# Attention stage of a two-layer model on one core: the state copy and the head gather move between engines, the scan units and value products are re-ordered

## The reference, cut to what matters

```python
def step(h, inp):                       # the scan of the Mamba block
    d_t, B_t, C_t, x_t = inp
    dA = jnp.exp(d_t[..., None] * A)
    dBx = d_t[..., None] * B_t[:, None, :] * x_t[..., None]
    h = h * dA + dBx
    y = jnp.sum(h * C_t[:, None, :], axis=-1)
    return (h, y)
...
A = jnp.einsum('bhnd,bhmd->bhnm', q, k) / jnp.sqrt(jnp.float32(Dm))
A = jnp.where(mask[None, None], A, -jnp.inf)
A = jax.nn.softmax(A, axis=-1)
sa = jnp.einsum('bhnm,bhmd->bnhd', A, v).reshape(Bm, Nm, Dm)
```

## Time and profile before

| | us |
|---|---|
| median of 3 runs | 2713.05 |
| the profiled execution | 2705.79 |
| its span | 2703.9 |
| TensorE busy | 2446.1 (90%) |
| VectorE busy | 2319.0 (86%) |
| ScalarE busy | 1859.3 (69%) |
| GpSimd busy | 1873.5 (69%) |

### The profile page before, as it was taken

How to read it: one execution, slowest core, us unless ns; L and a number is a source line. 1 busy time by engine, 2 the same in 40 slices (tenths; PEclk the granted TensorE clock), 3 DMA queues, 4 the chain that set the end, 5 groups by cost and what they waited for, 6 DMA issues and landing times. The chain is left out here.

```text
span 2703.9 us, 72872 instructions
## 1 busy us (share of the span) xinstructions
PE 2446.1 (90%) x29430; PEld 1463.3 (54%) x29430; DVE 2319.0 (86%) x2551; ACT 1859.3 (69%) x4077; POOL 1873.5 (69%) x1739
## 2 busy tenths in 40 slices
PE   7999999899777887899989999999999999999997
PEld 4444444333233334566656666666666666666665
DVE  6667778969898896899967899989998999899994
ACT  4555545466555553777767888888888888788883
POOL 2441142227767766677748899989998999999991
PEclk9999999999999998999989999999999999999999
DMA  3000000001121111030021112111211121111111
GB/s 104 9 9 9 9 7 9 8 23 40 49 49 44 49 47 39 7 94 14 12 64 47 38 31 66 37 32 35 62 33 36 35 62 40 29 32 37 33 22 38
DMA packets 171132, 97.57 MB, mean 36 GB/s; under 512 B 97155, under 2 KB 167791, under 8 KB 169263
## 3 DMA queue, kind: packets, MB, share of 16 engines
q1 hardware_dynamic: 170799, 92.91, 14.4%
HBM read 66.91 MB, written 7.08 MB: 27 GB/s over the span
## 5 line engine op out<-in xcount | busy, mean ns | idle before, releaser
L599 PE MATMUL ps<-xnT,qp 128*128 128x512 f32 (+3 forms) x1280 | 571.4, 565 | 28.4 <-ACT prob L814 28.3
L814 ACT ACTIVATE prob<-ps,mneg,shift 128x1024 f32<-128x1024 f32 (+7 forms) x384 | 366.3, 955 | 278.2 <-DVE mneg L720 277.3
L1902 DVE TENSOR_TENSOR area<-ps,tab 128x2048 f32<-128x2048 f32 x192 | 430.3, 2282 | 63.7 <-ACT area L1682 38.5
L720 DVE TENSOR_REDUCE mneg<-ps 128x1 f32<-128x1024 f32 (+7 forms) x384 | 341.1, 889 | 102.5 <-PE ps L599 101.6
L1413 PE MATMUL ps<-wqk,area 128*128 128x512 f32 x768 | 359.1, 610 | 27.9 <-DVE area L1968 22.4
L728 DVE STREAM_TRANSPOSE area<-prob 128x1024 f32<-128x1024 f32 (+7 forms) x384 | 354.1, 923 | 34.3 <-ACT prob L814 30.3
L2089 POOL TENSOR_TENSOR area<-area,rn 128x1024 f32<-128x1024 f32 x192 | 370.0, 1948 | 7.5
L1503 PEld LDWEIGHTS ps<-wvo,area 128*128 128x128 f32 x3072 | 355.2, 193 | 26.7 <-issue 20.9
L1503 PE MATMUL ps<-wvo,area 128*128 128x128 f32 x3072 | 361.9, 276 | 3.4 <-ACT area L1731 3.4
L599 PEld LDWEIGHTS ps<-xnT,qp 128*128 128x128 f32 x1280 | 222.2, 197 | 216.0 <-issue 167.0
L1724 ACT ACTIVATE ps<-ps,nmxl 128x64 f32<-128x64 f32 x1536 | 322.5, 344 | 5.1 <-DVE nmxl L1882 5.0
(11 more groups left out here) (273 smaller groups left out, 4445.1 us busy)
## 6 DMA issues: line engine op xcount, KB each, us to landing
xe<-bc_scratch SPq DMA_DIRECT2D x128, 128.0 KB, 3.1
area<-bc_scratch SPq DMA_DIRECT2D x128, 128.0 KB, 4.2
staged<-values_scratch SPq DMA_DIRECT2D x192, 32.0 KB, 1.9
wqk<-lwqk_dram SPq DMA_DIRECT2D x6, 1024.0 KB, 6.8
xp<-xc SPq DMA_DIRECT2D x96, 48.0 KB, 2.7
xc<-xs SPq DMA_DIRECT2D x96, 32.0 KB
wvT<-lwvT_dram SPq DMA_DIRECT2D x6, 512.0 KB, 8.1
wo<-lwo_dram SPq DMA_DIRECT2D x6, 512.0 KB, 9.7
```

Source lines behind the costliest of these rows:

```text
L599: mm = E.matmul(ps[:, r + o // 512, 0:w], k.qp[:, group % 2, i * P:(i + 1) * P], k.xnT[:, k0 + o:k0 + o + w], start=o // 512 != masked, st ...
L720: V.tensor_reduce(k.mneg[:, U:U + 1], of, X_AXIS, ALU.max, negate=True).then_inc(s("top"), 1)
L814: A.activation(k.prob[:, U % 2, 0:nk], ps[:, r:r + 2, :].rearrange("p a b -> p (a b)")[:, 0:nk], ACT.Exp, bias=k.mneg[:, U:U + 1], scale=k ...
L1902: V.tensor_tensor(k.rot[:, n % 2, w, :, :].rearrange("p c (h d) -> p c h d", d=DH), bcast(heads(what, n), 1, 2), bcast(k.tab[:, n % FRAME, ...
```

## The change

1. `shares`: the value products stand in whole groups of four: 4, 4, 4, 4, 4, 4, 8 for a square (before 4, 4, 4, 5, 5, 5, 5) and 0, 4, 4, 4, 4, 8, 8 for a triangle (before 2, 3, 4, 5, 5, 6, 7).
2. ScalarE's `values_out` is gone. VectorE turns the sums out of PSUM in 32 x 32 blocks (`turn_values`), and `gather` needs 4 products with the constant `pick` as the weights and 64 columns each, in place of 32.
3. The copy of the state moves from VectorE (L492) to ScalarE (`unit_state`), behind the exponential of the next step's odd piece; GpSimd's outputs wait for it.
4. GpSimd makes the input of unit u before the outputs of unit u - 1.
5. ScalarE makes the decay of unit u in the even piece of the same step, in place of the odd piece of the step before.
6. The scan starts at step 59 in place of 61, what prepares it comes one or two steps earlier, and the last two visits one step earlier.

```diff
-VISITS = {..., 50: ("dt", 0), 52: ("dt", 1), 98: ("mo", 0), 127: ("mo", 1)}
-FIRST_SCAN = 61
+VISITS = {..., 50: ("dt", 0), 51: ("dt", 1), 97: ("mo", 0), 126: ("mo", 1)}
+FIRST_SCAN = 59
...
-    return (4, 4, 4, 5, 5, 5, 5) if is_square(b) else (2, 3, 4, 5, 5, 6, 7)
+    return (4, 4, 4, 4, 4, 4, 8) if is_square(b) else (0, 4, 4, 4, 4, 8, 8)
...
 def unit_scan(k, u):
+    if c:
+        V.wait_ge(s("state"), u - NS + 1)
     for a in range(ET):
         ...
-    ins.then_inc(s("v"), k.v.up())
-    V.wait_ge(s("v"), k.v.n)
-    V.tensor_copy(k.last[:, i, :], k.hx[:, b, :, CH - 1]).then_inc(s("scanned"), 1)
+    ins.then_inc(s("scanned"), 1)
+
+def unit_state(k, u):
+    A, s = k.ac, k.sem
+    A.wait_ge(s("scanned"), u + 1)
+    A.activation(k.last[:, u % NS, :], k.hx[:, u % 2, :, CH - 1], ACT.Copy).then_inc(s("state"), 1)
...
     def gather(b):
         E.wait_ge(s("ot"), b + 1)
-        for i in range(NTH):
-            for q in range(4):
-                mm = E.matmul(ps[WIN * q:WIN * (q + 1), 6 + b % 2, 256 + DV0 * i:256 + DV0 * (i + 1)], k.oT[:, b % 2, WIN * i:WIN * (i + 1)],
-                              k.pick[:, DV0 * q:DV0 * (q + 1)], start=True, stop=True, skip_group_check=True)
+        of = k.oT[:, b % 2, :].rearrange("p (i q v) -> p q i v", q=4, v=DV0)
+        for q in range(4):
+            mm = E.matmul(ps[WIN * q:WIN * (q + 1), 6 + b % 2, 256:256 + DV0 * NTH], k.pick[:], of[:, q, :, :], start=True, stop=True, skip_group_check=True)
...
+    def turn_values(b):                       # VectorE, after the maximum in the first slot of batch b + 2
+        V.wait_ge(s("value_mm"), b + 1)
+        if b >= 2:
+            V.wait_ge(s("pick_mm"), b - 1)
+        V.transpose(k.oT[:, b % 2, :], ps[:, 6 + b % 2, 0:WIN * NTH]).then_inc(s("ot"), 1)
...
-        if i == 0 and b >= 2:                 # ScalarE
-            values_out(b - 2)
-        elif i == 2 and b >= 2:
+        if i == 2 and b >= 2:
             gathered(b - 2)
         j = step_of(U)
         if j is not None:
             branch(j)
-        elif U >= FIRST and scanned_in(step_of(U - 1) + 1) is not None:
-            A.wait_ge(s("half_pool"), at["pool"]["du"])
-            unit_decay(k, scanned_in(step_of(U - 1) + 1))
+            if scanned_in(j) is not None:
+                A.wait_ge(s("half_pool"), at["pool"]["du"])
+                unit_decay(k, scanned_in(j))
+        elif U >= FIRST and scanned_in(step_of(U - 1) - 1) is not None:
+            unit_state(k, scanned_in(step_of(U - 1) - 1))
...
     def outputs(u):                           # GpSimd
+        G.wait_ge(s("state"), u + 1)
         unit_outputs(k, u)
...
             branch(j)
+            if scanned_in(j) is not None:
+                unit_inputs(k, scanned_in(j))
             if scanned_in(j - 1) is not None:
                 outputs(scanned_in(j - 1))
-            if scanned_in(j) is not None:
-                unit_inputs(k, scanned_in(j))
```

More of the change, by code:

```diff
@@ L343, in up @@
         return 1
-VISITS = {8: ("sa", 0), 10: ("out", 0), 17: ("hat", 0), 19: ("in", 0), 21: ("in", 1), 23: ("in", 2), 25: ("in", 3), 47: ("xd", 0), 50: ("dt", 0), 52: ("dt", 1),
-          98: ("mo", 0), 127: ("mo", 1)}
-FIRST_SCAN = 61
+VISITS = {8: ("sa", 0), 10: ("out", 0), 17: ("hat", 0), 19: ("in", 0), 21: ("in", 1), 23: ("in", 2), 25: ("in", 3), 47: ("xd", 0), 50: ("dt", 0), 51: ("dt", 1),
+          97: ("mo", 0), 126: ("mo", 1)}
+FIRST_SCAN = 59
 TAP_ROWS = range(22, 45)
@@ L486, in unit_scan @@
         ins = V.tensor_tensor_scan(h, k.dc[:, b, a, :], h, k.last[:, i, a:a + 1] if c else 0.0, ALU.mult, ALU.add)
-    if c + 1 == NCH:
-        ins.then_inc(s("scanned"), 1)
-        return
-    ins.then_inc(s("v"), k.v.up())
-    V.wait_ge(s("v"), k.v.n)
-    V.tensor_copy(k.last[:, i, :], k.hx[:, b, :, CH - 1]).then_inc(s("scanned"), 1)
+    ins.then_inc(s("scanned"), 1)
[3 more added lines that the diff above has]
+    A.activation(k.last[:, u % NS, :], k.hx[:, u % 2, :, CH - 1], ACT.Copy).then_inc(s("state"), 1)
 def unit_outputs(k, u):
@@ L790, in attention_dve @@
             continue
+        if U % NTH == 0 and U // NTH >= 2:
+            turn_values(U // NTH - 2)
         if 0 < U < NTH:
@@ L797, in attention_dve @@
             unit_scan(k, scanned_in(step_of(U - 1)))
+    turn_values(NB - 2)
+    turn_values(NB - 1)
     V.wait_ge(s("combined"), 2 * len(COMBINE) + 4)
@@ L826, in experts @@
         A.activation(k.xe[:, 4 * half:4 * half + 4, :].rearrange("p e m -> p (e m)"), of, ACT.Copy).then_inc(s("xe"), 1)
[L828 to L833, removed]
     def gathered(b):
@@ L886, in branch @@
             A.preload_act_table_set("natural_log_exp_and_others")
-        elif j == 54:
+        elif j == 52:
             softplus("abs", 0)
             softplus("exp", 0)
-        elif j == 55:
+        elif j == 53:
             softplus("ln", 0)
             softplus("abs", 1)
-        elif j == 56:
+        elif j == 54:
             softplus("exp", 1)
@@ L922, in attention_act @@
             branch(j)
-        elif U >= FIRST and scanned_in(step_of(U - 1) + 1) is not None:
-            A.wait_ge(s("half_pool"), at["pool"]["du"])
-            unit_decay(k, scanned_in(step_of(U - 1) + 1))
+            if scanned_in(j) is not None:
[3 more added lines that the diff above has]
+            unit_state(k, scanned_in(step_of(U - 1) - 1))
     weights(len(COMBINE) + 1, COMBINE_LAST, H0)
-    values_out(NB - 2)
     gathered(NB - 2)
-    values_out(NB - 1)
     gathered(NB - 1)
@@ L1029, in branch @@
             G.tensor_copy(k.tail[:], k.mxp[:, :, TH:TH + PAD]).then_inc(s("half_pool"), ev.up("tail"))
-        elif j in (56, 57):
-            rate(j - 56)
+        elif j in (54, 55):
+            rate(j - 54)
         elif j == 48:
@@ L1037, in branch @@
             ins.then_inc(s("half_pool"), ev.up("y"))
-        elif j == 58:
+        elif j == 56:
             G.wait_ge(s("half_pool"), ev.n)
@@ L1071, in attention_pool @@
     part_shares(COMBINE_LAST, H0)
-    output("mo", 1)
     combine(len(COMBINE) + 1, COMBINE_LAST, H0 - 1, NB - 2)
@@ L1731, in mix_out @@
         A.activation(k.mixT[:, :, 2 * i:2 * i + 2, :].rearrange("p c w q -> p w c q"), pair(f"mix{i}", n).rearrange("p w (c q) -> p w c q", q=WIN), ACT.Copy).then_inc(s("mixT"), 1)
[L1733 to L1737, removed]
     def normal_turned(m):
@@ L1830, in transformer_act @@
             if u // NS + 1 < NCH:
-                state(u)
+                unit_state(k, u)
         if new_frame(n + 1) and n + 1 < NTILE:
@@ L1980, in scan @@
         if u >= UNITS // 2 + NS:
-            V.wait_ge(s("state"), u - NS - UNITS // 2 + 1)
+            V.wait_ge(s("state"), u - NS + 1)
         for a in range(ET):
@@ L2152, in transformer_pool @@
             if u // NS + 1 < NCH:
-                G.wait_ge(s("state"), u - UNITS // 2 + 1)
+                G.wait_ge(s("state"), u + 1)
             unit_outputs(k, u)
```

## The result

The changed kernel takes 2645.5 us (median of 4 runs, 2644.13 to 2648.06) against 2712.3 before (here the median of 4 runs): ratio 0.9755, 95% interval 0.9733 to 0.9776, 67 us less. Forecast were 2653 and a range of 2618 to 2688. A second timing, in another set of runs, gave 0.9766 (0.9749 to 0.9782). The profiled execution took 2648.06.

The account below looks back on a forecast made before the run. Attention stage bound by TensorE early, VectorE under taps, a scan-GpSimd ring in triangles and VectorE in squares under the scan. Terms 20 + 10 + 15 + 4 + 9.5 = 58 us off, giving 2653 us, range 2618 to 2688.

Parts of the forecast that it names:

- the two mechanisms: Attention stage: gains from both TensorE's part and a part of the ring, 35 to 80 us, chance 0.60.
- Value products: TensorE's value slots: whole groups stream fewer columns, saving 1.0 us a triangle and 1.2 us a square.
- Gather: TensorE's gather: four products of 64 columns replace 32, saving 0.3 us (0 to 0.45).
- A turn from PSUM: VectorE's added turn of 256 columns: costs 0.38 us (0.25 to 0.7) a batch and waits for nothing.
- The ring is cut: Scan stretch: scans no longer wait for GpSimd's input; 2.0 us per square and triangle, 15 us in all.
- the turns: Scan stretch: GpSimd's operations and scans alternate; triangle units take 4.7, 5.9, 5.5 and 7.1 us.
- State copy on ScalarE: Behind the odd exponential: it just fits, 2.3 against 2.26 us; GpSimd's L500 starts some 0.45 us behind the scan.
- The slower rival: ScalarE's state copy comes late, delaying GpSimd's outputs; at a 1.4 us lag 2732 us, chance 0.04.
- Work at chunk ends: GpSimd's gate, shares and combine leave the ring: 4 us taken of 9 us in all.
- The early scans: Two scans moved early, ahead of the scan stretch: partly hidden in the 3 us gain of batches 28 to 31.
- The end: Last batches: scans and the wait for the gate go, 8.5 us, plus 1 for bare gathers and turns.
- Taps: Batches 22 to 26, VectorE full with convolution taps: each pays 0.38 us for the turn, 2 us in all.

Follow-up runs that it names:

- e1_groups: The kernel before with only the whole groups of four value products; 2683.8 us, ratio 0.9909.
- e6_outputs_first: The changed kernel with GpSimd's outputs of unit u - 1 again before the input of unit u; 2670.6 us, ratio 0.9864.
- e8_short_outputs: The changed kernel with GpSimd's outputs in the attention stage cut to 32 of 256 columns, the others left out; 2613.8 us, ratio 0.9651.
- e7_start_61: The changed kernel with the scan starting at step 61 and visits and preparations where they were before; 2646.6 us, ratio 0.9773.
- e3_products: The kernel before with whole groups, VectorE's turn and the gather of four products, scan order as before; 2673.6 us, ratio 0.9874.
- e10_stage_late: e9_spread_act with SyncE's fetch of values at the seventh piece, not the third, from batch 30 on; 2626.6 us, ratio 0.9709.
- e9_spread_act: The changed kernel with the spreading of values (L948) from batch 30 on made by ScalarE, not GpSimd; 2639.8 us, ratio 0.9749.
- e5_copy_back: The changed kernel with the state copy back on VectorE, GpSimd's new order kept; 2659.9 us, ratio 0.9822.

## Why the prediction was right

The time and its sign were right, and so were the two mechanisms. That the time came within 8 us is in part luck. By the first turns of the batches, the gains were, with the forecast in brackets: batches 1 to 15 21 (20), batches 16 to 27 6.4 (7), batches 28 to 31 -4.5 (+3), batches 32 to 45 22.0 (15 + 4, less the little of it that falls into batch 46), from batch 46 on 11.5 (9.5); 0.8 was lost ahead of batch 1. One term had the wrong sign, and others that were too small made up for it. By its steps:

- **Value products, 1.0 us a triangle and 1.2 a square.** Right. The slots of whole groups cost what their columns said, and in e1_groups an early triangle falls from 17.1 to 16.1.
- **Gather, 0.3 (0 to 0.45).** The mechanism was right, the term too small: 0.41. With the products an early batch loses 1.5, not 1.3; over batches 1 to 15 that is about the 20 of the sum.
- **A turn from PSUM, 0.38.** It took 0.42 with 0.07 under the next, 0.35, and waited for nothing.
- **The ring is cut, 2.0 us for two batches.** Right in mechanism, but a third too small: (25.3 + 23.9) - (23.4 + 22.9) = 2.9. The triangle came as worked out, unit by unit, to 0.3. The square is 0.6 better, because its units take 6.1, 5.8 and 5.8, not 6.3, 5.9 and 5.9, and the last 5.7. e6_outputs_first and e8_short_outputs show both halves, the ring and the turns.
- **State copy on ScalarE.** It fitted behind the exponential. The slower rival did not come: L504 follows a square's scan by 726.94 - 726.63 = 0.31.
- **Work at chunk ends, 4.** Hardly anything of this came; the larger gain of the ring hides it. With the ring it makes 61 x (6.30 - 5.95) = 21 us against 15 + 4. But at 3.0 us a pair (the batches 36 and 37 together take 49.3 before and 46.3 changed) the ring alone gives 7 x 3.0 = 21 of the 22.0 in batches 32 to 45. What these 14 batches take beyond seven such pairs, 353.8 - 7 x 49.3 = 8.7 us before, is still 331.8 - 7 x 46.3 = 7.7.
- **The early scans, "partly hidden in the 3".** This step of the sum failed. Batches 28 to 31 were to gain 3 and lost 4.5. I took 2.6 off TensorE's 5.6 for four turns and the two scans as VectorE's work and left out that the scans would be held back by GpSimd's. The first three scans of the changed kernel, in the last step of the square 30 and the first two of the triangle 31, show it:

```profile
600.04 3.76 DVE L488 TENSOR_TENSOR_SCAN area<-area 128x256 f32<-128x256 f32 x2
605.63 3.30 DVE L488 TENSOR_TENSOR_SCAN area<-area 128x256 f32<-128x256 f32 x2
611.50 2.54 DVE L488 TENSOR_TENSOR_SCAN area<-area 128x256 f32<-128x256 f32 x2
```

 They take 3.76, 3.30 and 2.54, not 1.4, and lie 5.6 and 5.9 apart, as under the scan. e7_start_61, without the two units there, gains 4.3 us in the same batches: a unit costs there 8.8 / 2 = 4.4.
- **The end, 9.5.** It gave 11.5, of which 4.7 in batch 46. The last visit waits no more for its gate. One thing was overlooked: its products take 2.05 us in place of 3.45.

```profile
982.25 2.05 PE L646 MATMUL ps<-wout,area 128*128 128x128 f32 x16
```

 The windows over these products (columns as in rows 2), first before, then changed, show the granted clock at 0.55 and at 1.00 of full speed:

```profile
1037.40:1040.80 3.40, 3.40 (x19) 3.17 (x19) 2.19 (x3) 1.19 (x2) 0.00 (x0) 0.55 0.00 0
```

```profile
982.25:984.25 2.00, 2.00 (x23) 1.88 (x20) 1.38 (x3) 1.55 (x4) 0.00 (x0) 1.00 0.03 8
```

 Before, TensorE had stood idle for the 3.46 us of the wait; at 0.55 it was mostly at 1.2 GHz, the lower of its two levels. So the wait cost TensorE its own length and 1.4 us more behind it. e7_start_61 shows that this gain and the loss of the step above belong together: the two units were moved from the end to the front, and the time stayed.
- **Taps, 0.38 for each of five batches.** A side effect was missed: the spreading L948 now falls on other taps. One pair of taps in batch 23 took 4.22 us, where the same place before took 2.58; e3_products has it too, so it comes with the products.

```profile
442.95 4.22 DVE L761 SCALAR_TENSOR_TENSOR wqT<-wqk,taps,wqT 128x1024 f32<-128x1024 f32 x2
```

 L948 starts at 444.19 there. It is in the sum of batches 16 to 27, which gained about 6 where 7 were forecast.

What stays open: the 3 us by which e3_products exceeds its two halves, why the chunk ends gave only 1 us, and the 2 us by which the transformer stage is shorter, which is within the spread of the runs.

## What to carry to other kernels

When a wait between two engines is taken away, look at what they share: work that the wait kept apart will now overlap, and where it shares a way it is done by turns. What is won is then less than the wait: here some 44 us of waiting went and 33 us came back inside the scans. The next gain came from moving work off that way (e8_short_outputs, e10_stage_late). A unit moved to another stretch can cost there far more than its work on the one engine that was counted (here 4.4 us in place of 1.4). And when work changes engines, look at every queue that waits for its result: e9_spread_act lost most of its gain to a fetch that stood ahead of others in SyncE's queue.

## What the runs showed of the hardware

- A scan with both inputs in SBUF and GpSimd's tensor operations exclude each other almost fully and alternate when both are ready: a pair of scans of 1.38 us takes 3.29 beside L506 and L476, and L476 grows from 1.29 to 1.50. The Trainium skill (SBUF — State Buffer, 🔬 SBUF: two separate sides) calls it an exclusive lock held for the whole instruction; the lengths of the scans agree to within some 0.2 us a collision, but GpSimd's instructions grow by only 0.2 to 0.4 us, less than the 0.69 of a whole scan.
- Other VectorE instructions grew beside GpSimd's too: a copy of 128 x 2 elements took 310 ns on average in place of 196 (e5_copy_back), a pair of taps (beside L948) 4.22 us in place of 2.58.
- Four products of 64 columns in four quarters of the array hold TensorE for 0.14 us, less than the 0.25 that I had made of wider ones.
- Eight products of 128 columns (x16 in their row) took TensorE 3.45 us at a granted clock of 0.55, behind 3.46 us of idle time. Behind 3.55 us in which it was never idle (978.70 to 982.25, changed kernel) they took 2.05 at 1.00.
